# Expert stage of an attention and mixture-of-experts layer: row transposes by TensorE or by DMA

## The reference

```python
xf = x.reshape(-1, D)                       # 4096 tokens of 256
scores = xf @ router_w.T                    # 8 experts
top_v, top_i = jax.lax.top_k(scores, 2)
routing_w = jax.nn.softmax(top_v, axis=-1)
for e in range(8):
    w_e = jnp.sum(jnp.where(top_i == e, routing_w, 0.0), axis=-1)
    h = jax.nn.gelu(xf @ expert_w1[e].T, approximate=False)   # 256 -> 1024
    out = out + h @ expert_w2[e].T * w_e[:, None]             # 1024 -> 256
```

## Time and profile before

| | |
|---|---|
| median of 3 runs | 806.88 us (804.73 to 807.64) |
| the profiled execution's own time | 809.17 us |
| its span, first to last instruction | 807.4 us |
| TensorE busy, of the span | 720.1 us, 89% |
| VectorE, ScalarE, GpSimd busy | 473.7, 441.5, 414.9 us |
| DMA of GpSimd's queue, of 16 engines' span | 20.46 MB, 15.8% |
| DMA of SyncE's queue | 35.15 MB, 14.2% |
| chain that ended last | TensorE 52%; L383 26%, L1150 24%, L1117 2% |

### The profile page before, as it was taken

How to read it: one execution, slowest core, us unless ns; L and a number is a source line. 1 busy time by engine, 2 the same in 40 slices (tenths; PEclk the granted TensorE clock), 3 DMA queues, 4 the chain that set the end, 5 groups by cost and what they waited for, 6 DMA issues and landing times.

```text
span 807.4 us, 22860 instructions
## 1 busy us (share of the span) xinstructions
PE 720.1 (89%) x7008; PEld 588.6 (73%) x7009; DVE 473.7 (59%) x1494; ACT 441.5 (55%) x1231; POOL 414.9 (51%) x442
## 2 busy tenths in 40 slices
PE   0898999999999894649999999999999999999993
PEld 0576666666666562537998999999899999989982
DVE  3797999999999887952444433443433344343331
ACT  2676888878888772534444444444444444444441
POOL 2465776776776662452544454454455444445523
PEclk9898999999999997788999999999999999999998
DMA  5233334334334320001322322332332332233222
GB/s 155 87 109 103 118 104 143 117 107 140 117 106 142 110 60 27 7 13 41 46 44 47 52 48 50 52 44 42 51 52 45 52 46 44 45 52 51 47 28 26
DMA packets 40122, 55.93 MB, mean 69 GB/s; under 512 B 5600, under 2 KB 33504, under 8 KB 40096
## 3 DMA queue, kind: packets, MB, share of 16 engines
q0 software_dynamic: 14976, 20.46, 15.8%
q1 hardware_dynamic: 25120, 35.15, 14.2%
HBM read 36.71 MB, written 18.87 MB: 69 GB/s over the span
## 4 chain that ended last, share of the span: by engine, by line
PE 52%; DMA 1%; issue 1%; POOL 0%; DVE 0%; ACT 0%; POOLq 0%; DVEq 0%
PE bank L383 26%; PE bank L1150 24%; PE bank L1117 2%; DMA out<-attn,rows_to 1%; POOL out L1092 0%; DMA xin<-xn_rows,rows_from 0%; DVE stage L1214 0%; ACT stage L1170 0%; DVE attn L1230 0%; POOL xin L1078 0%; DVE rows_from L1207 0%; DVEq L1198 0%; POOLq L308 0%; POOLq L307 0%; POOLq L1100 0%
## 5 line engine op out<-in xcount | busy, mean ns | idle before, releaser
L383 PE MATMUL bank<-stage,w1h 128*128 128x256 f16 x1248 | 207.9, 274 | 1.5 <-DVE stage L1214 1.5
L1150 PE MATMUL bank<-w2h,pt 128*128 x624 | 170.1, 273 | 1.6 <-DVE spare L1221 1.6
L383 PE MATMUL bank<-stage,w1l 128*128 128x256 f16 x624 | 170.7, 274 | 0.0
L1150 PE MATMUL bank<-w2h,spare 128*128 x624 | 170.1, 273 | 0.0
L1150 PE MATMUL bank<-w2l,pt 128*128 x624 | 170.1, 273 | 0.0
L1187 ACT ACTIVATE pt<-ss 128x512 f16<-128x512 f32 x78 | 44.8, 621 | 175.9 <-PE bank L1150 175.9
L383 PEld LDWEIGHTS bank<-stage,w1h 128*128 x1248 | 122.5, 98 | 16.5 <-issue 1.9
L1092 POOL DMA_INDIRECT out<-res,rows_to x40 | 63.8, 1594 | 107.8 <-DVE rows_from L1207 48.3
L1092 POOL DMA_INDIRECT out<-attn,rows_to x38 | 60.7, 1596 | 98.4 <-DMA out<-attn,rows_to 57.8
L1214 DVE SCALAR_TENSOR_TENSOR stage<-bank,stage 128x512 f16<-128x512 f32 x39 | 26.9, 690 | 118.3 <-ACT stage L1170 118.3
L1181 ACT ACTIVATE spare<-bank 128x512 f32<-128x512 f32 x78 | 46.6, 597 | 54.8 <-PE bank L383 54.8
(11 more groups left out here) (209 smaller groups left out, 1722.3 us busy)
## 6 DMA issues: line engine op xcount, KB each, us to landing
stage<-w1c SPq DMA_DIRECT2D x16, 512.0 KB, 3.7
stage<-w2c SPq DMA_DIRECT2D x16, 512.0 KB, 3.7
xin<-x SPq DMA_DIRECT2D x32, 128.0 KB, 2.1
xn_rows<-xn SPq DMA_DIRECT2D x32, 128.0 KB, 1.7
xb<-x SPq DMA_DIRECT2D x32, 128.0 KB, 3.3
out<-res SPq DMA_DIRECT2D x32, 128.0 KB, 3.5
xin<-xn_rows,rows_from POOLq DMA_INDIRECT x40, 2.8
out<-res,rows_to POOLq DMA_INDIRECT x40, 3.8
```

Source lines behind the costliest of these rows:

```text
L383: ins = pe.matmul(dst, lhs(a, k), rhs(c, k), start=(n == 0), stop=(n == len(terms) - 1))
L1150: ins = pe.matmul(bY[h][:, 0:D], (hh, hl)[a][:, f, h * P:(h + 1) * P], (w2h, w2l)[c][:, DS(which * (FC * D) + f * D, D)], start=(f == a == ...
```

## The change

The first two groups are handled as before. For every other group the order is turned round: ScalarE and VectorE first split the gathered rows as they stand, in SBUF, into `rh[n]` and `rl[n]` (f16, in `stage[1]`), two instructions of 128 x 256 each in place of one of 128 x 512 that read PSUM. SyncE then issues H x KC x 2 = 8 transposing DMAs for the group, each of 128 x 128 f16 (32 KB), from `rh`/`rl` into `xh`/`xl`. They are released by two waits, on `h3` of two groups before (TensorE has read `xh` and `xl`) and on `xgl_in` (both parts are written), and each adds 16 to `turned[n]`, for which TensorE waits in `first`. The splits are made for group j+3 in step j (j+2 before), the gathers for j+4 (j+3 before). A gather waits for the low part of the group that held its buffer, no longer for the transposes of it. TensorE has no transposes but the eight of the first two groups. The loop covers 17 turns instead of 18, and the last five steps are written out. The number of bytes gathered and scattered is the same.

```diff
+        rh = [view(stage[1], m * D, H, D, dt=F16) for m in range(2)]
+        rl = [view(stage[1], (2 + m) * D, H, D, dt=F16) for m in range(2)]
...
+        TURNS = 16 * 2 * H * KC
...
+            @block.sync
+            def _(sp):
+                def turn_rows(i, m):
+                    if isinstance(i, int) and i == 0:
+                        sp.sem_inc(turned[m], TURNS)
+                        return
+                    n, _k = slot(i, m, 0)
+                    sp.wait_ge(e["h3"], upto(i, m, -2))
+                    sp.sem_inc(e["turnable"], 1)
+                    sp.wait_ge(e["xgl_in"], upto(i, m))
+                    sp.sem_inc(e["turning"], 1)
+                    for c in range(KC):
+                        for rows, xt in ((rh[n], xh[n]), (rl[n], xl[n])):
+                            for h in range(H):
+                                sp.dma_start(xt[:, c, h * P:(h + 1) * P], rows[:, h, c * P:(c + 1) * P],
+                                             transpose=True).then_inc(turned[n], 16)
+
+                groups(sp, turn_rows, first=2)
...
-                    wait_rows(e["xgt"])
+                    wait_rows(e["xgl_in"])
...
-                    gather(i, m, 3)
+                    gather(i, m, 4)
...
                     pe.wait_ge(e["xgl_in"], upto(i, m, ahead))
+                    pe.wait_ge(turned[n], TURNS * (k + 1))
...
                     first(i, m, 1)
-                    turn_rows(i, m, 2)
-
...
-                    n, _k = slot(i, m, ahead)
-                    act.wait_ge(e["xgt"], upto(i, m, ahead))
-                    act.wait_ge(e["h3"], upto(i, m, ahead - 2))
-                    act.activation(xh[n].rearrange("p k n -> p (k n)"), bX[:], ACT.Copy,
-                                   scale=XS).then_inc(e["xgh_in"], 1)
+                    n, k = slot(i, m, ahead)
+                    act.wait_ge(gathered[n], 16 * (H * k + H))
+                    act.wait_ge(turned[n], TURNS * k)
+                    for h in range(H):
+                        ins = act.activation(rh[n][:, h, :], xg[n][h][:, 0:D], ACT.Copy, scale=XS)
+                    ins.then_inc(e["xgh_in"], 1)
...
-                    rows_hi(i, m, 2)
-
-                rows_hi(0, 0, 0)
-                gelu(0, 0, 0, between=lambda: rows_hi(0, 1, 0))
+                    rows_hi(i, m, 3)
+
+                turned_hi(0)
+                gelu(0, 0, 0, between=lambda: turned_hi(1))
+                rows_hi(0, 2, 0)
...
                     dve.wait_ge(e["xgh_in"], upto(i, m, ahead))
-                    dve.scalar_tensor_tensor(out=xl[n].rearrange("p k n -> p (k n)"), in0=bX[:], scalar=XS,
-                                             in1=xh[n].rearrange("p k n -> p (k n)"),
-                                             op0=ALU.mult, op1=ALU.subtract).then_inc(e["xgl_in"], 1)
+                    for h in range(H):
+                        ins = dve.scalar_tensor_tensor(out=rl[n][:, h, :], in0=xg[n][h][:, 0:D], scalar=XS,
+                                                       in1=rh[n][:, h, :], op0=ALU.mult, op1=ALU.subtract)
+                    ins.then_inc(e["xgl_in"], 1)
...
-                    rows_of(i, m, 3)
+                    rows_of(i, m, 4)
...
-                    rows_lo(i, m, 2)
+                    rows_lo(i, m, 3)
```

## The result

The changed kernel takes 799.4 us (median of 8 runs, 797.7 to 803.6) against 806.8 us before (8 runs beside them, 804.7 to 809.5): a ratio of 0.991, with a 95% interval of 0.989 to 0.994. It is faster, by 7.4 us where 15.9 were forecast. The profiled execution took 798.0 us with a span of 796.3.

What follows compares the result with a forecast made beforehand. It took TensorE's stream to bound the expert stage. The sum was -16.3 us from TensorE and 0 from ScalarE, VectorE, SyncE, GpSimd, start and end: a median of 790.6, given as 791.0 us, range 788 to 850.

Steps and rivals of the forecast that it cites:

- the view it started from: Expert stage: TensorE busy throughout, so a microsecond taken from its stream is worth a microsecond until another engine bounds.
- four transposes: TensorE's stream: 37 groups lose 0.44 us each, 16.3 us in all; the period falls from 10.91 to 10.48 us.
- ScalarE's and VectorE's new pieces: Splits in SBUF: high part 0.83 us, low part 0.80 us, covered by over 5 us free in a group; cost 0.
- GpSimd's loop: Scatters and gathers of a group: 9.99 us at the shortest, 10.39 with the lengthening taken, just under 10.48; cost 0.
- x: Lengthening of GpSimd's loop by scatters landing later beside the transposes: 0.4 us taken, 3.4 at the far end.
- Rivals 1 and 2: GpSimd's loop becomes the bound: partly, giving 799 us (chance 0.13), or costing more than TensorE gives, 847 to 899 (0.15).
- rival 1: GpSimd's loop partly the bound, x between 0.5 and 0.9 us: 8 us gained, 799 us; chance 0.13.
- t: SyncE's time from one transposing DMA to the next: 0.5 to 0.9 us taken, up to 2.2 for the range.
- Rival 3: SyncE's transposes don't overlap one another, t above 1.36 us; at 2.2 us 248 us slower, 1054 us; chance 0.16.
- Two of the signs that were given for the forecast: In the profile: SyncE's eight issues take under 10 us, and SyncE waits between groups.
- The start: First transposed group: free for t up to 0.75 us, at 1.3 late by 4.4 us, once; nothing taken.
- The loop: Eight transposes must fit into a group: t up to 1.31 us for the whole gain, break-even 1.36 us.

Runs made afterwards that it cites:

- four: Changed kernel with each group's eight transposes cut into four of 128 x 256 (64 KB), same bytes: 790.7 us, ratio 0.979; once more 790.1 us, 0.978.
- none: Changed kernel with the transposes of groups 2 to 38 left out, SyncE only raising the semaphore (output wrong): 792.9 us, ratio 0.981.
- the second profile: The changed kernel itself measured and profiled once more, with nothing altered: 797.1 us, ratio 0.988 to the kernel before.
- warm: Changed kernel with 36 useless matmuls filling TensorE's wait for the first transposed group, to keep the clock up: 798.8 us, ratio 0.989.
- three: Changed kernel with the first three groups transposed by TensorE instead of the first two, SyncE beginning with group 3: 794.4 us, ratio 0.983.
- two: Changed kernel with two transposes of 128 x 512 (128 KB) a group in place of eight, same bytes: 789.7 us, ratio 0.978.
- plain: Changed kernel with the eight DMAs of a group copying their blocks without transposing (output wrong): 788.5 us, ratio 0.980.

## Why the prediction was right and wrong

Right: the view it started from. TensorE's stream was the bound, four transposes were worth 0.44 us a group, and in four the whole gain came out: 0.979 of 806.8 is 789.9, 16.9 us less. ScalarE's and VectorE's new pieces took 0.71 and 0.80 us, against 0.83 and 0.80 worked out. GpSimd's loop, the nearest other bound in the prediction, didn't move: on the average x was 0.02 us (3.05 to 3.07), where 0.4 was taken and 0.49 could be borne. In four it was 0.2 (58.0 us in 18 waits), and that could be borne too. Rivals 1 and 2 did not come about, though 0.28 of the chance stood on them. The measured 799 us is also the number that rival 1 names, but that is chance, as GpSimd was not the bound. Range and sign held.

Wrong: the forecast time, by over half of the gain (7.4 us of 15.9). The step that failed is the one that priced t, the time from one transpose to the next. It had bounds of 0.49 and 2.2 us and took 0.5 to 0.9, because plain transfers are issued every 0.49 us while in flight together. That is true of plain ones (0.60 us here), but the transposing instruction holds SyncE itself for 1.23 us, so overlap in flight doesn't help. Rival 3 had named just this, that nothing shows transposes overlapping as plain copies do, but put its price above 1.36 us. Two of the signs that were given for the forecast failed with it: the eight issues took over 10 us, and SyncE did not wait between groups but once. It was the only operation of the change that the trace of before doesn't show, and it got a value near one end of its range (a factor of four wide), although both the start and the loop turned on it.

Two terms followed from this one. The start: the prediction had written that at 1.3 us the first transposed group would be 4.4 us late, once, and then took nothing; it was 22.1 - 17.75 = 4.3 us late. That the two agree so well is partly luck: 0.8 us of it is the one issue of 2.00 us, and about 0.5 the first block of the stage, which took longer than before as it did in none. The loop: the threshold was set at 10.48 / 8 = 1.31 us with nothing for what SyncE does between two groups, 0.3 us a group. With it the threshold is 1.27, just what was measured, and the group takes 10.50 us against 10.48. Not foreseen at all was the clock: after 3.8 us idle, the next block took 3.0 us longer, and 1.6 us longer after 3.5 us idle in the second profile. In the profile of after the three terms are 3.8 (group 2 at 22.1 against 18.3 in none), 3.0 and 1.4 us, together the 8.2 that lie between it and none; most of the loss is at the start. But they are not three independent losses. SyncE's chain of 296 transposes, 390 us long, has no slack to make up for a late start, and when the start was mended in warm and three, TensorE waited later in the stage. The whole gain came where the chain was cut to about half (four, two, plain).

The Trainium skill's figure (VectorE: DVE Perf Modes, The three transpose paths: 1309 ns for a 128 x 128 two-byte transpose by DMA) is close to the 1.27 us from start to start in this trace. The prediction cited it, worked out 10.47 us from it, and let the row of the plain transfers decide, which is the wrong neighbour. The runs add what the figure doesn't say: it is a cost per instruction on the issuing engine, the same from 16 to 128 KB. The Trainium skill's advice (VectorE: DVE Perf Modes, Rules for kernel authors) to take TensorE for a 128 x 128 transpose where a destination in PSUM will do is not borne out here, as TensorE was the bound: in four the DMA path is 2% faster.

What stays open: why an issue now and then takes 1.4 to 2.5 us instead of 1.23. In the changed kernel, its second profile, three and warm they stand in the first four and the last three groups that are turned by DMA, and with so little slack they decide how much TensorE waits. No run was made on it. They are not what makes the two profiles of the changed kernel differ by 2 us at group 38, since they add up to 2.5 us in both; 1.4 us of that is the block of group 2 (8.25 and 6.81 us), and why its clock differed is open too.

## What to carry to other kernels

When work is moved to an idle queue, price the issuing engine's time for each instruction, and if the trace has no instruction of that kind, take the whole range seriously: here one unknown price of 0.5 to 2.2 us decided both the start and the loop. Count what the issuing engine does between two groups as well, and leave slack for issues that take longer: at 10.50 us against 10.48 there was none. If a cost is per instruction, fewer and larger instructions get the gain back; cutting 8 into 4 was worth as much as moving the work in the first place. And a wait that disappears at one place proves nothing as long as the chain that caused it is as long as before: compare where the last item begins.

## What the runs showed of the hardware

- A transposing DMA within SBUF held SyncE for 1.23 us whether it moved 16 or 32 KB, for 1.24 with 64 KB and for 1.26 with 128 KB, and now and then for 1.4 to 2.5; a plain copy of 32 KB within SBUF held it for 0.60 us. From the start of the issue to landing it was 2.4 us (changed) and 5.0 us (three) for the last of a group's eight of 32 KB, and 4.5 us for the last of four of 64 KB.
- 256 KB of transposes a group raised the DMA share of the stage from 0.30 to 0.46; the wait for a scatter's landing was 3.05 us on the average before, 3.07 after, 3.03 with the transposes left out and 3.22 with four of 64 KB.
- After 3.8 us of idle TensorE the granted clock was 0.50 over the next 3.36 us and 0.65 over the block of 8.25 us, 3.0 us longer than usual; after 3.5 us idle it was 0.79 over a block of 6.81 us; with the idle time filled (warm) it was 1.00 and the block took 5.41.
- From one group of eight issues to the next SyncE needed 0.33 and 0.59 us in turn for two waits, two semaphores and, in every other one, the branch of the loop (warm, three).
